# A state-space and expert kernel on one Trainium2 core: TensorE forms the scan product before the product of C and B, and GpSimd makes the low parts of the expert weights in sixteen pieces

## The reference, cut to what matters

```python
xdt = xh * dtc[..., None]
Y_diag = jnp.einsum('bcln,bcsn,bhcls,bcshp->bclhp', Cc, Bc, Lmat, xdt)
...
Y = (Y_diag + Y_off + xh * D[:, None]).reshape(Bsz, L, D_INNER)
Y = Y * jax.nn.silu(z)
Y = Y * jax.lax.rsqrt(jnp.mean(Y * Y, axis=-1, keepdims=True) + EPS) * norm_w
```

```python
h1 = jnp.einsum('nc,ehc->neh', flat, w1)
h3 = jnp.einsum('nc,ehc->neh', flat, w3)
h = jax.nn.silu(h1) * h3
```

## Time and profile before

| | us |
|---|---|
| median of three runs | 1245.38 |
| lowest and highest of the three | 1243.94, 1248.22 |
| the profiled execution, whole | 1249.54 |
| its span, first to last instruction | 1247.8 |
| TensorE busy, share of the span | 1053.5, 84% |
| VectorE busy, share | 846.9, 68% |
| ACT busy, share | 712.4, 57% |
| GpSimd busy, share | 400.6, 32% |

### The profile page before, as it was taken

The page is one execution under the profiler, slowest core; times in us unless marked ns, Lnnn a source line. Parts: engine busy times, 40 slices in busy tenths (PEclk is TensorE's granted clock), DMA queues, the critical chain, the costliest instruction groups (busy, mean ns, idle before and its releaser), DMA issues. The chain is left out here.

```text
span 1247.8 us, 23207 instructions
## 1 busy us (share of the span) xinstructions
PE 1053.5 (84%) x6746; PEld 925.6 (74%) x6746; DVE 846.9 (68%) x2117; ACT 712.4 (57%) x1560; POOL 400.6 (32%) x413
## 2 busy tenths in 40 slices
PE   2999999999995946899999975567609999899998
PEld 2988889898884924566666665566509999899997
DVE  5576767667667636999999964799854555445554
ACT  4466564655652238888888853666504555455554
POOL 4232232322314600001000001457662444524444
PEclk9999999999996567788788876788658999999999
DMA  4121212112100022123212302735234544333331
GB/s 157 60 69 44 85 42 82 44 44 82 34 1 24 1 72 62 40 68 68 64 47 60 68 1 83 233 112 160 82 128 122 150 127 126 95 96 96 99 95 56
DMA packets 82778, 99.14 MB, mean 79 GB/s; under 512 B 9483, under 2 KB 68626, under 8 KB 82554
## 3 DMA queue, kind: packets, MB, share of 16 engines
q1 hardware_dynamic: 72490, 74.31, 22.0%
q0 software_dynamic: 8752, 21.25, 4.9%
q10 hardware_dynamic: 1440, 2.40, 0.6%
HBM read 72.30 MB, written 27.02 MB: 80 GB/s over the span
## 5 line engine op out<-in xcount | busy, mean ns | idle before, releaser
L1616 PE MATMUL e_p_y<-w,e_gT 128*128 (+1 forms) x852 | 118.2, 275 | 0.0
L1563 DVE TENSOR_TENSOR e_g<-e_sl,e_p_h 128x342 f32<-128x342 f32 x142 | 72.6, 511 | 63.5 <-ACT e_sl L1541 55.5
L877 POOL TENSOR_TENSOR m_rs<-m_ms,m_minus_half 128x4 f32<-128x4 f32 x16 | 18.6, 1164 | 300.5 <-ACT m_ms L910 300.5
L1616 PEld LDWEIGHTS e_p_y<-w,e_gT 128*128 128x128 f32 (+1 forms) x852 | 106.1, 191 | 0.4 <-issue 0.4
L1545 ACT ACTIVATE e_gT<-e_p_gx 128x384 f32<-128x384 f32 x142 | 69.6, 490 | 63.9 <-PE e_p_gx L1606 63.9
L87 PE MATMUL e_p_h<-w_hi,e_xT_hi 128*128 x284 | 104.5, 368 | 1.5 <-DVE e_g L1563 0.8
L1541 ACT ACTIVATE e_sl<-e_p_h 128x342 f32<-128x342 f32 x142 | 64.8, 457 | 69.7 <-PE e_p_h L89 69.5
L1567 DVE TENSOR_TENSOR e_xT_lo<-e_p_gx,e_xT_hi 128x128 fp32r<-128x128 f32 x142 | 41.4, 292 | 86.2 <-ACT e_xT_hi L1549 85.9
L1527 POOL DMA_INDIRECT sorted_scratch<-e_xg x71 | 69.0, 972 | 91.2 <-DVE e_xg L1573 89.6
L1525 POOL DMA_INDIRECT out<-e_xg x71 | 68.9, 970 | 85.9 <-DVE e_xg L1573 79.9
L968 DVE SCALAR_TENSOR_TENSOR m_c<-m_p_x,m_vecs,m_c 128x506 f32<-128x506 f32 (+2 forms) x144 | 95.5, 735 | 0.0
(11 more groups left out here) (357 smaller groups left out, 3356.3 us busy)
## 6 DMA issues: line engine op xcount, KB each, us to landing
e_xg<-sorted_scratch SPq DMA_DIRECT2D x142, 130.0 KB, 2.1
m_cum<-cum_scratch SPq DMA_DIRECT2D x16, 1024.0 KB
g_adjT<-in_adjT SPq DMA_DIRECT2D x16, 512.0 KB, 4.0
g_adj<-in_adj SPq DMA_DIRECT2D x16, 512.0 KB
c_adjT<-in_adjT SPq DMA_DIRECT2D x16, 512.0 KB, 6.5
x_tokens<-in_x SPq DMA_DIRECT2D x16, 256.0 KB, 5.0
sorted_scratch<-nothing SPq DMA_DIRECT2D x2, 1040.0 KB, 10.1
sorted_scratch<-nothing SPq DMA_DIRECT2D x12, 130.0 KB, 2.6
```

The source lines that it names most:

```text
L1563: dve.tensor_tensor(g[:, i % D3], sl[:, i % 2], p_h3[i % 2][:, 0:HP], ALU.mult).then_inc(q["g_ready"], 1)
L1616: last = pe.matmul(p_y[d % 2][:, 0:P], gT[0:r, d % D3, k], w2k[:, bass.ts(e, P)], start=k == 0, stop=k == len(CH) - 1)
```

## The change

Two edits. In the TensorE program of the state-space stage the block of the product of C and B moves behind the block of the scan product; both keep their conditions. In the GpSimd program of the routing stage the subtraction that makes the low part, one operation over 128 x 8 x 341 elements for each of `w1` and `w3`, becomes eight operations over 128 x 341, each with its own increment of the semaphore, and the final wait counts sixteen.

```diff
                     last.then_inc(q["xh_done"], 1)
-                if live(d):
-                    pe.wait_ge(q["xdt_ready"], d + 1)
-                    pe.wait_ge(q["B_ready"], d + 1)
-                    pe.wait_ge(q["C_ready"], d + 1)
-                    for g in range(G):
-                        l0 = g * N
-                        pe.matmul(p_hG[:, g, 0:N], Bt[:, d % 2, l0:l0 + P], Ct[:, d % 2, l0:l0 + N], start=True, stop=True)
-                        last = pe.matmul(p_hG[:, g, N:NB], Bt[:, d % 2, l0 + P:l0 + N], Ct[:, d % 2, l0 + P:l0 + N], start=True, stop=True)
-                    last.then_inc(q["G_done"], 1)
                 if live(v):
                     pe.wait_ge(q["zs_ready"], min(s + 1, STEPS))
                     need(pe, q["y1_ready"], 2 * (v - 0))
...
                     last.then_inc(q["Y_done"], 1)
+                if live(d):
+                    pe.wait_ge(q["xdt_ready"], d + 1)
...
+                    last.then_inc(q["G_done"], 1)
...
                     pool.wait_ge(q["w_hi"], 4 + n + 1)
-                    pool.tensor_tensor(dst.lo[:, :, 0:H], raw[n], dst.hi[:, :, 0:H].bitcast(F32), ALU.subtract).then_inc(q["w_split"], 1)
+                    for e in range(EX):
+                        pool.tensor_tensor(dst.lo[:, e, 0:H], raw[n][:, e], dst.hi[:, e, 0:H].bitcast(F32), ALU.subtract).then_inc(q["w_split"], 1)
...
-            pool.wait_ge(q["w_split"], 2)
+            pool.wait_ge(q["w_split"], 2 * EX)
```

More of the change, by code:

```diff
@@ L1041, in _ @@
                     last.then_inc(q["Y_done"], 1)
+                if live(d):
+                    pe.wait_ge(q["xdt_ready"], d + 1)
+                    pe.wait_ge(q["B_ready"], d + 1)
+                    pe.wait_ge(q["C_ready"], d + 1)
+                    for g in range(G):
+                        l0 = g * N
+                        pe.matmul(p_hG[:, g, 0:N], Bt[:, d % 2, l0:l0 + P], Ct[:, d % 2, l0:l0 + N], start=True, stop=True)
+                        last = pe.matmul(p_hG[:, g, N:NB], Bt[:, d % 2, l0 + P:l0 + N], Ct[:, d % 2, l0 + P:l0 + N], start=True, stop=True)
+                    last.then_inc(q["G_done"], 1)
 BF16 = mybir.dt.bfloat16
```

## The result

The changed kernel takes 1248.98 us in the median of 19 runs (1246.95 to 1253.40), the kernel before 1245.38 us in 19 runs beside it (1242.84 to 1249.44). The ratio is 1.0031, with a 95% interval of 1.0019 to 1.0042: slower by 3.9 us (2.4 to 5.2). The forecast was 1253.8, slower by 8.4: its direction is right and its size is more than twice what was measured. The profiled execution of the changed kernel took 1248.29 us, with a span of 1246.5.

The account below looks back on a forecast made before the run. The state-space stage was read as loops of nearly equal length, the present loss being TensorE's own order (17.36 against 16.79 us a step). Order +6.1 and pieces +2.3 gave +8.4 on 1245.4: 1253.8 us, range 1236 to 1263.

Parts of the forecast that it names:

- part 1: State-space stage, TensorE: the scan product put ahead of the product of C and B; together +6.1 us (−11.0 to +16.2).
- x is freed: TensorE is done before the taps and waits about 3.0 us before x, the three matmuls opening its step.
- the tap loop: State-space step from x through transposes, `xdt` and nine taps to the next x: 16.23 us, becoming 16.23 + d = 18.11.
- d: Time x loses per step by starting slow after its wait: between 0 and 2.65 us, taken as 1.88.
- twelve steps: State-space steps from x at 497.23 to x at 705.60: 12 × 18.11 = 217.3 against 208.4 us, +8.9.
- first x to the fourth: Head of the state-space steps: the first x of the twelve steps comes 1.3 us earlier, −1.3.
- the last step and the tail: End of the state-space stage: last step's taps after slow x +1.9, scan product beginning earlier in the tail −3.4.
- The difference carries over: The profiled execution lay 4.2 us over the median; the priced difference was taken to hold for the median, 1245.4, all the same.
- Part 2: Routing stage: two GpSimd subtractions become sixteen pieces; VectorE taken to wait for all eight of a set, +1.15 × 2 = +2.3 us.
- Fast x: Rival, state-space steps: x stays fast after its wait, d = 0, sum −8.7, 1236.7 us; chance 0.20.
- The transfer of `cum`: Rival, state-space steps: `cum` binds as steps get even, taking 8 us off the fast-x gain, about 1245; chance 0.03.
- The rival in which VectorE is let in: Routing: VectorE enters after the first piece, saving 7.3 us; with x slow 1244.2 us, no change; chance 0.10.

Follow-up runs that it names:

- e3: Changed kernel plus twelve 128x128 products that nothing reads, between the transposes and the scan product; 1240.08 us, 0.9947 of the kernel before.
- e2: Kernel before with only the subtraction in eight pieces, TensorE's order as before; 1243.67 us, ratio 0.9978.
- e6: Kernel before with the three matmuls opening a TensorE step sent in thirds, the first waiting for all but the last two taps; ratio 0.9989.
- e7: Kernel before with the subtraction in sixteen pieces, half an expert each; ratio 0.9955.
- e8: Kernel before with the subtraction in two pieces of four experts each; ratio 1.0008.
- e9: Kernel before with the subtraction in eight pieces, each behind a wait that has long been met; ratio 0.9991.
- e10: Kernel before with GpSimd's bias addition in four pieces of 128x128, nothing else; ratio 1.0003.
- e1: Changed kernel with the subtraction back in one operation, so only TensorE's new order; 1250.13 us, 1.0033 of the kernel before.
- e4: Kernel before plus eight products that nothing reads, between the transposes and the product of C and B; 1242.28 us, ratio 0.9958.
- e5: Changed kernel with the three matmuls opening a TensorE step sent in thirds, the first waiting for all but the last two taps; 0.9907 of the kernel before.

## Why the prediction was wrong in size

**What bounds it, and the mechanism of part 1: right.** The wait for `xdt` is gone, x is freed, a wait of 2.90 us (3.0 forecast) stands before it, its clock falls, and the tap loop is 16.23 + d. The ten steps from 528.93 on, 18.19 each against 18.11, make d 1.96 in place of 1.88; x took 4.78 us there in the mean, 1.94 more than 2.84. (The 17.98 of all twelve is lower by the one step of 15.20.) The forecast said that x came only after waits of none, 4.31 and 9.12 us. The trace has one more, the first, at 447.49, which took 4.93 us after a wait of 0.78 and 1.19 us of other work, with 4.16 us of waiting before that. It speaks for a slow x too. The rule of the Trainium skill that I weighed, in "TensorE: Matmul & The Clock Gate", "HAM oscillation — how this bites in real kernels", told the direction, and the trace agrees: 2.90 us of waiting ahead of every burst, 4.37 to 5.49 us in place of 2.84 at its start. Experiment 3 shows the cause, by taking the wait away and leaving the order.

**The terms of part 1: +6.1 forecast, +4.1 measured.** The traces of experiments that leave TensorE's program alone allow a better baseline than one execution. Seven have the old order in the steps' final form (before, e2, e6 to e10; e6 starts x early only where it waits), two the new (changed, e1). The old ones fall into two kinds. The three traces with a step of 20 us (before, at 582.26; e2, e6) have 208.4 to 208.6 us in the twelve steps, and these executions lay 4.2, 5.2 and 7.6 us over their kernels' medians. The four without it (e7 to e10) have 204.0 to 205.1 and lay between 2.6 under and 0.6 over. Of the new order, the changed kernel's lay 0.7 under its median and e1's 3.8 over.

| stretch | old: the profile I used | old: mean of 7 (range) | old: mean of the 4 | new: changed, e1 | forecast |
|---|---|---|---|---|---|
| first x to the fourth | 49.7 | 48.6 (46.4 to 49.7) | 48.2 | 47.7, 47.7 | −1.3 |
| twelve steps | 208.4 | 206.2 (204.0 to 208.6) | 204.6 | 215.8, 215.7 | +8.9 |
| last x to routing | 61.5 | 62.3 (61.5 to 63.3) | 62.3 | 56.0, 60.2 | −1.5 |
| all | 319.6 | 317.1 (313.1 to 320.6) | 315.1 | 319.5, 323.6 | +6.1 |

All seven against both give −0.9 for the head, +9.5 for the steps and −4.2 for the end, in sum +4.4. The four against the changed kernel, typical executions against a typical one, give −0.5, +11.2 and −6.2, in sum +4.5. Either sum agrees with the 4.1 measured, and in either the term that was most mis-sized is *the last step and the tail*, +1.9 − 3.4 = −1.5, which came out at −4.2 to −6.2. Against the profile that I used, in three stretches, the changed kernel first and e1 second: from the last x to the last transposes 26.0 and 25.6 us in place of 23.1 (+2.7 in the mean for +1.9); from there to the last Y 11.8 and 12.5 in place of 17.0 (−4.9 for −3.4); from the last Y to the routing stage 18.2 and 22.1 in place of 21.4, where I had nothing and where the two runs of the new order differ for the most part by the clock under that last Y, shown above.

**"The difference carries over" was wrong, and luck hid it.** I noted that the profiled execution lay 4.2 us over the median and kept its 208.4 us as the baseline of the steps. The table shows where the difference sits: 3.8 us of it are in the twelve steps, against the 204.6 of the four typical traces. The new order doesn't have those longer steps: it takes 215.8 and 215.7 us in an execution under its median and in one over it. So against a typical execution the steps cost 11.2 us and not 8.9: the new steps were taken 1.5 too long, the old ones 3.8. That the end gave back more than forecast is what kept the sum of part 1 below the forecast and not above it.

**Part 2: the step that failed.** "So I take it that VectorE waits for all eight: +1.15 × 2 = +2.3 us." Alone it measured −2.7 us (−4.5 to −1.1), and the traces show −1.2 and −1.3. It rested on one row, L1369 at 841.74. That row was read rightly, and was the wrong one to carry over: three of three such cases were held in the kernel before, yet in the traces with eight or sixteen pieces each operation of the chain that met a piece entered at the next boundary, nine or ten times a run. The sign against the forecast that I had named, this operation under 1 us during the subtractions, is there: 0.47 and 0.39. I had written down the other bound as well, "if the four VectorE operations behind it each wait for a piece too, about nothing", and this is what happened: the waits above 0.16 us each, 0.3 + 4 × 0.67 = 3.0 us, and 2.9 in the second set, against 4.64 and 3.56 us before, are 2.4 us less. The first chain also asks 1.0 us later, 3.44 us after its bias addition in place of 2.41, which leaves 1.3. I gave that mechanism no chance of its own, only the one in which VectorE is freed by the first piece, −7.3, and two pieces (e8) show that it is not: the second operation waits for the second piece in full.

"SBUF — State Buffer", "SBUF: two separate sides", of the Trainium skill says that the pair of ports goes to one of the two engines for a whole instruction. The traces agree with it: each of the waits listed here ends with a GpSimd instruction, the long ones that pass over boundaries too. Taken by itself it promised 7.3 us only because I let one instruction of the chain pay and not all five.

**The sum.** +4.1 and −1.3 to −2.7 make +1.4 to +2.8; the whole change measured +3.9 (2.4 to 5.2). Within their intervals these agree; no contact between the parts was seen.

**The rivals.** Fast x (1236.7) did not happen, but it names the size of the prize: with the wait filled the first steps are 16.8 us, the 16.79 that I had worked out for d = 0, until TensorE itself becomes the bound. The transfer of `cum` did not bind: 5.4 us in six waits, and 4.2 in five with the wait filled (e3). The rival in which VectorE is let in gave 1244.2 by a gain of 7.3, which is refuted too.

## What to carry to other kernels

A move that frees an engine early does not shorten the loop by itself: ask what stands behind the new wait, and in what state the engine starts it. Here the remedy was a finer condition in the new order, the first third of x started two taps early; in the old order the same condition gave nothing that could be told. Where two engines share a port, count every link of a chain of small operations against the size of the other's piece: five links and eight pieces of 0.87 us gain little, sixteen smaller pieces gain more, two nothing. And take a baseline of several executions where steps alternate, or one whose time is the median: the trace used here lay 4 us over it, and nearly all of that sat in the one stretch whose change was being priced.

## What the runs showed of the hardware

- TensorE's clock was 0.50 at the start of x after waits of 2.90 us (638.53 to 641.50 in the changed kernel), and x then took 4.37, 4.54 and 5.49 us in turn. After waits of 1.11 us (e4) x took 2.84 each time. Between these it went either way: 4.54 us after a wait of 1.21 (e3), 2.84 after one of 1.51 (e4, e7), and after waits of 1.68 to 2.00 us (e5) 2.81 in five steps running and 4.36 to 4.51 in the next six, in the same loop.
- Products that nothing reads made the kernel faster: by 0.8% of its time in the new order (1.0031 to 0.9947) and by 0.4% in the old (0.9958).
- A VectorE operation of 0.17 us beside back-to-back GpSimd pieces of 0.87 us takes 0.83 us, each time anew; beside pieces of 0.51 us, 0.45 to 0.49. In a few places an operation was passed over, at two boundaries (e10) and at four (e7).
